# Linear-attention layers: the product of query and key sum moved from ScalarE to GpSimd, and a longer lag between blocks

## The chip, the cores and the metric

One core of a Trainium2 chip runs the whole program. The metric is the time on the device of one execution, in microseconds, as the median of several. The engines are named as in the profile: PE (TensorE's matmuls), PEld (its weight loads), DVE (VectorE), ACT (ScalarE), POOL (GpSimd), SP (SyncE, which issues the DMAs here).

## The reference

The program is a chain of twelve stages on x of shape 16 x 256 x 128: four "macaron" sandwiches, each half an FFN, an attention, half an FFN. The change touches one stage, the linear-attention layers (`attn1`), eight layers one after the other:

```python
for i in range(8):                       # 8 layers, 16 heads of 64
    residual = x
    Q  = elu(x @ Wq[i] + bq[i]) + 1
    Kf = elu(x @ Wk[i] + bk[i]) + 1
    V  = x @ Wv[i] + bv[i]
    KV, sumK = sum_s(Kf * V), sum_s(Kf)  # over the 256 positions of a sequence
    Z   = 1 / (Q * sumK + 1e-6)
    att = Q * KV * Z
    x = layer_norm(gelu(att @ Wo[i] + bo[i]) + residual) * ln1_s[i] + ln1_b[i]
    h = gelu(gelu(x @ W1[i] + b1[i]) @ W2[i] + b2[i])
    x = layer_norm(h + x) * ln2_s[i] + ln2_b[i]
```

## The kernel before

Everything is float32. A group is 512 tokens (`GT`), which is two sequences (`NQ`) of 256; there are 8 groups (`G`) and 8 layers, so 64 turns. The activations stay in SBUF, transposed (`zT`: 128 channels by tokens). The 1024 columns of heads are cut in 8 blocks (`NB1`) of 128, so that one block of one group is a tile of 128 x 512.

Each engine has its own program; they meet at semaphores only (`Ev` counts: `wait` asks that a step is done, `wait_free` that a buffer is free again). `over_layers` runs a list of parts in each slot, one slot for each group; a part has a lag, and in slot s it works on group s - lag. At the head of each pair of slots it calls `opening`, which on ACT loads the table set with exp and ln (L1790). The list is made at the end of `steps`: for each block position w from 0 to 7 it appends

- PE: `proj_pe(w)` (three matmuls, for keys, queries, values, L1488), then `out_pe(w - 3)` (L1502), which adds a block's attention times Wo into bank 6;
- ACT: `exp_act(w)` (exp of keys L1549, relu of keys L1550, exp of queries L1553), then `inv_act(w - 1)`: 1/(Q sumK + tiny) as exp(-ln(.)), one ln for each of the two sequences with the key sum as its scale (L1563), and one exp over 512 columns (L1568);
- DVE: `feature_dve(w)`: key feature and its sum, one instruction for each sequence (L1621), min(exp, 1) - 1 of the queries (L1629), max with q + b (L1632), values times key features and their sum (L1638, twice); then `att_dve(w - 2)`: Q times KV times Z (L1652, twice);
- POOL: `query_pool(w - 1)`: adds the 1 to the query features (L1690).

A negative block index wraps to the last blocks of the group before. At w = 2, when the last block of the group before has been added, the MLP is appended: on PE `mlp_pe` (L1515, L1521; for the group two slots back), on ACT the load of the gelu table (L1573), `y_act` (L1579, for the group one slot back), `h_act` (L1588, L1592) and the load of the exp table (L1596), on POOL the two residual additions (L1698, L1702). At w = 3 follow the transposes and norm statistics (L1529, L1663, L1668), at w = 4 POOL's reciprocal roots (L1711, L1714), at w = 5 the norm's application on DVE (L1677), at w = 6 the transposes back (L1538) and ACT's copies `back_act` (L1605, L1609). Weights of the next layer are loaded by SP while a layer runs.

The ring buffers of the attention are four deep (`a1_qf`, `a1_ksum`, `a1_kv`, `a1_z`, `a1_att`), those of the exponentials and key features two.

## Time and profile before

| | us |
|---|---|
| median of 3 runs (lowest, highest) | 6160.44 (6157.66, 6160.94) |
| the profiled execution | 6133.33 |
| its span, first to last instruction | 6131.5 |
| linear-attention layers within the span | about 1390 to 4277 |

The profiled execution is one of its own, 27 us below the median. The page gives each engine's busy time over the whole span; the linear-attention layers are slices 10 to 28 of its 40. A timeline row gives the start of an instruction in us from the span's start, its length, how many of the kind follow each other, and in brackets how long the engine sat idle before it and who released it. Instructions of one engine overlap a little, so that a pair of 0.48 us each may take 0.88 together.

### The profile page before, as it was taken

To read this page: it belongs to the slowest core of one execution; us is meant where nothing else is said; L and a number is where in the kernel's file an instruction comes from. 1 tells how busy PE (TensorE), PEld (TensorE's weight loads), DVE (VectorE), ACT (ScalarE), POOL (GpSimd) and SP (SyncE) were. 2 spreads that over 40 slices of the span, in tenths; PEclk is the share of its full clock that TensorE was granted. 3 is DMA by queue.
4 is the path that set the end of the run, shared out by engine and by line. 5 is a ranking of instruction groups with operands and counts; after the bars stand their busy time and mean duration, and the time that the engine had idled before them with its cause. 6 is when DMAs were issued, how large, how long until landed. Compare 5 with 4: busy or idle time off the path is not lost.

```text
span 6131.5 us, 75002 instructions
## 1 busy us (share of the span) xinstructions
PE 4957.9 (81%) x19882; PEld 2885.5 (47%) x19882; DVE 3793.3 (62%) x11610; ACT 2984.0 (49%) x5250; POOL 1120.8 (18%) x1540
## 2 busy tenths in 40 slices
PE   4788888848888888888888888888587559999964
PEld 2677777733333333333333333333354336665543
DVE  4555445567767667676677667676656744444466
ACT  1100000018878777787777878777122124444421
POOL 1000000022222222222222222222200012322210
PEclk8888888869999999999999999999798679999976
DMA  1000000000000000000000000000000023222300
GB/s 45 1 1 1 1 1 1 1 18 1 1 18 1 14 4 11 7 1 18 0 14 4 5 13 1 18 0 0 0 0 0 0 31 47 45 42 40 47 1 14
DMA packets 161144, 71.60 MB, mean 12 GB/s; under 512 B 64565, under 2 KB 158474, under 8 KB 160650
## 3 DMA queue, kind: packets, MB, share of 16 engines
q1 hardware_dynamic: 160778, 67.65, 6.4%
q8 instruction: 117, 1.92, 0.1%
q14 instruction: 249, 2.04, 0.1%
HBM read 55.89 MB, written 11.73 MB: 11 GB/s over the span
## 4 chain that ended last, share of the span: by engine, by line
PE 48%; DVE 24%; issue 13%; ACT 8%; SPq 3%; DMA 2%; POOL 1%; DVEq 1%; ACTq 0%; POOLq 0%
PE bank L1488 7%; PE bank L1521 4%; PE bank L1502 4%; PE bank L1210 3%; DVE arena L1652 3%; DVE arena L1638 3%; PE bank L1515 3%; SPq L2048 3%; PE bank L2107 3%; PE bank L1207 3%; PE bank L2167 3%; DVE arena L1621 2%; PE bank L1199 2%; DVE arena L1277 2%; DVE arena L1663 2%
## 5 line engine op out<-in xcount | busy, mean ns | idle before, releaser
L1488 PE MATMUL bank<-arena 128*128 (+1 forms) x3072 | 1474.1, 617 | 14.7 <-ACT arena L1550 13.1
L1488 PEld LDWEIGHTS bank<-arena 128*128 128x128 f32 x3072 | 599.4, 199 | 745.2 <-issue 710.0
L1621 DVE SCALAR_TENSOR_TENSOR arena<-arena 128x256 f32<-128x256 f32 x1024 | 391.8, 421 | 777.5 <-ACT arena L1550 773.3
L1502 PE MATMUL bank<-arena 128*128 128x512 f32 x1024 | 566.4, 636 | 219.2 <-DVE arena L1652 217.9
L1563 ACT ACTIVATE arena<-arena,const_table 128x256 f32<-128x256 f32 x1024 | 558.7, 601 | 78.9 <-POOL arena L1690 78.8
L1690 POOL TENSOR_SCALAR arena<-arena 128x512 f32<-128x512 f32 x512 | 316.7, 619 | 1356.7 <-DVE arena L1632 1349.3
L1638 DVE SCALAR_TENSOR_TENSOR arena<-bank,bv,arena 128x256 f32<-128x256 f32 x1024 | 450.4, 478 | 0.0
L1652 DVE SCALAR_TENSOR_TENSOR arena<-arena 128x256 f32<-128x256 f32 x1024 | 448.7, 480 | 0.7 <-issue 0.7
L2118 DVE TENSOR_REDUCE arena<-bank 128x2 f32<-128x512 f32 x256 | 176.9, 691 | 419.8 <-PE bank L2109 419.7
L1502 PEld LDWEIGHTS bank<-arena 128*128 128x128 f32 x1024 | 168.2, 191 | 556.6 <-DVE arena L1652 501.9
L1549 ACT ACTIVATE arena<-bank,bqk 128x512 f32<-128x512 f32 x512 | 350.0, 684 | 162.6 <-PE bank L1488 129.6
L1632 DVE SCALAR_TENSOR_TENSOR arena<-bank,bqk,arena 128x512 f32<-128x512 f32 x512 | 384.4, 751 | 18.1
L2151 ACT ACTIVATE arena<-bank 128x512 f32<-128x512 f32 x256 | 152.9, 597 | 479.1 <-PE bank L2140 479.1
L1515 PE MATMUL bank<-arena 128*128 128x512 f32 x512 | 283.7, 683 | 118.6 <-ACT arena L1588 117.6
L1553 ACT ACTIVATE arena<-bank,bqk 128x512 f32<-128x512 f32 x512 | 352.2, 688 | 8.9 <-PE bank L1488 8.6
L1550 ACT ACTIVATE arena<-bank,bqk 128x512 f32<-128x512 f32 x512 | 347.9, 680 | 0.5 <-issue 0.5
L1568 ACT ACTIVATE arena<-arena 128x512 f32<-128x512 f32 x512 | 322.7, 630 | 16.2
L2107 PE MATMUL bank<-const_table,arena 128*128 128x256 f32 x1024 | 324.1, 410 | 3.4 <-issue 2.1
L1277 DVE TENSOR_TENSOR arena<-arena,bank 128x512 f32<-128x512 f32 x352 | 227.6, 685 | 136.7 <-PE bank L1210 136.7
L2094 POOL TENSOR_TENSOR arena<-arena 128x256 f32<-128x256 f32 x256 | 185.4, 724 | 647.4 <-DVE arena L2084 647.4
L332 ACT ACTIVATE xT<-bank 128x512 f32<-128x512 f32 x64 | 38.2, 597 | 510.1 <-PE bank L327 479.5
L1210 PE MATMUL bank<-arena 128*128 128x128 f32 x1536 | 281.1, 276 | 0.0
(340 smaller groups left out, 8923.2 us busy)
## 6 DMA issues: line engine op xcount, KB each, us to landing
arena<-packed_dram SPq DMA_DIRECT2D x432, 64.0 KB
packed_dram<-arena SPq DMA_DIRECT2D x48, 192.0 KB, 2.1
arena<-in_L_attn_Wk_dram SPq DMA_DIRECT2D x16, 256.0 KB, 3.0
arena<-in_L_attn_Wq_dram SPq DMA_DIRECT2D x16, 256.0 KB, 3.8
arena<-in_L_attn_Wv_dram SPq DMA_DIRECT2D x16, 256.0 KB, 4.3
arena<-in_L_attn_Wo_dram SPq DMA_DIRECT2D x8, 512.0 KB, 3.5
arena<-in_L_attn_W_dram SPq DMA_DIRECT2D x16, 256.0 KB, 2.9
out_dram<-x SPq DMA_DIRECT2D x1, 2048.0 KB, 8.7
```

The lines of the kernel that those rows point to most:

```text
L1210: last = nc.tensor.matmul(bank[:, 4 + 3 * c, h * P:(h + 1) * P], a0_X[:, c, h, :], a0_It[:, c, h, :] if k else ident, start=True, stop=True)
L1277: last = nc.vector.tensor_tensor(dst[:, c, :, :], old, four(bank[:, 3 + i + 3 * c, :]), ALU.subtract)
L1488: nc.tensor.matmul(bank[:, RING1[m % 5], :], w1p[k][:, i * P:(i + 1) * P], zT_of(g), start=True, stop=True).then_inc(a1_proj.sem, 1)
L1502: nc.tensor.matmul(bank[:, 6, :], wo1[:, i, :], a1_att[:, i % 4, :], start=(i == 0), stop=(i == NB1 - 1)).then_inc(a1_outd.sem, 1)
L1515: nc.tensor.matmul(bank[:, i % 2, :], w1a[:, i * P:(i + 1) * P], a1_x1[:], start=True, stop=True).then_inc(a1_h_psum.sem, 1)
L1553: nc.scalar.activation(a1_eq[:, i % 2, :], q, ACT.Exp, bias=bqk[:, 1, i:i + 1])\
L1563: last = nc.scalar.activation(seqs(a1_z[:, i % 4, :])[q], seqs(a1_qf[:, i % 4, :])[q], ACT.Ln, bias=table[:, C_TINY:C_TINY + 1], scale=a1_ ...
L1621: last = nc.vector.scalar_tensor_tensor(seqs(a1_kf[:, i % 2, :])[q], seqs(a1_ek[:, i % 2, :])[q], 1.0, seqs(a1_kf[:, i % 2, :])[q], ALU.mi ...
L1632: nc.vector.scalar_tensor_tensor(a1_qf[:, i % 4, :], b[1], bqk[:, 1, i:i + 1], a1_eq[:, i % 2, :], ALU.add, ALU.max)\
L1638: last = nc.vector.scalar_tensor_tensor(seqs(a1_kv_terms[:])[q], seqs(b[2])[q], bv1[:, i:i + 1], seqs(a1_kf[:, i % 2, :])[q], ALU.add, ALU ...
L1652: last = nc.vector.scalar_tensor_tensor(seqs(a1_att[:, i % 4, :])[q], seqs(a1_qf[:, i % 4, :])[q], a1_kv[:, i % 4, q:q + 1], seqs(a1_z[:, ...
L2107: nc.tensor.matmul(dst, a3_R[:, w % 4, i * P:(i + 1) * P], table[:, C_KEYS:C_KEYS + T], start=True, stop=False)
```

## The change

The two logarithms of a block, which took the key sum as their scale, become one logarithm over 512 columns without a scale, in place in `a1_z`. Its argument, the query feature times the key sum, is now made by POOL in `query_pool`: behind its addition of 1 it waits for that, and multiplies each of the two sequences by its key sum with a pointer operand (`a1_qs` tells ACT). The wait for a free buffer moves from ACT to POOL, and DVE gets one more, ahead of L1632. The lags along the blocks grow by one: `inv_act(w - 2)`, `att_dve(w - 3)`, `out_pe(w - 4)`; `query_pool(w - 1)` keeps its own. The MLP and all that follows it move from w = 2, 3, 4, 5, 6 to w = 3, 4, 5, 6, 7.

```diff
--- before.py
+++ after.py
@@ -1405,6 +1405,7 @@
             a1_kfd = ev("a1_kfd", per=NB1)
             a1_qmin = ev("a1_qmin", per=NB1)
             a1_qfd = ev("a1_qfd", per=NB1)
+            a1_qs = ev("a1_qs", per=NB1)
             a1_ln = ev("a1_ln", per=NB1)
             a1_inv = ev("a1_inv", per=NB1)
             a1_attd = ev("a1_attd", per=NB1, credit=4, by="vector")
@@ -1557,13 +1558,9 @@
                 def inv_act(i):
                     def fn(g, u):
                         t = turn(g)
-                        a1_qfd.wait(nc.scalar, t, i + 1)
-                        a1_attd.wait_free(nc.scalar, t, i + 1)
-                        for q in range(NQ):
-                            last = nc.scalar.activation(seqs(a1_z[:, i % 4, :])[q], seqs(a1_qf[:, i % 4, :])[q],
-                                                        ACT.Ln, bias=table[:, C_TINY:C_TINY + 1],
-                                                        scale=a1_ksum[:, i % 4, q:q + 1])
-                        last.then_inc(a1_ln.sem, 1)
+                        a1_qs.wait(nc.scalar, t, i + 1)
+                        nc.scalar.activation(a1_z[:, i % 4, :], a1_z[:, i % 4, :], ACT.Ln,
+                                             bias=table[:, C_TINY:C_TINY + 1]).then_inc(a1_ln.sem, 1)
                         a1_ln.wait(nc.scalar, t, i + 1)
                         nc.scalar.activation(a1_z[:, i % 4, :], a1_z[:, i % 4, :], ACT.Exp, scale=-1.0)\
                             .then_inc(a1_inv.sem, 1)
@@ -1629,6 +1626,7 @@
                         nc.vector.tensor_scalar(a1_eq[:, i % 2, :], a1_eq[:, i % 2, :], 1.0, -1.0, ALU.min, ALU.add)\
                             .then_inc(a1_qmin.sem, 1)
                         a1_qmin.wait(nc.vector, t, i + 1)
+                        a1_attd.wait_free(nc.vector, t, i + 1)
                         nc.vector.scalar_tensor_tensor(a1_qf[:, i % 4, :], b[1], bqk[:, 1, i:i + 1],
                                                        a1_eq[:, i % 2, :], ALU.add, ALU.max)\
                             .then_inc(a1_read["q"].sem, 1)
@@ -1688,6 +1686,13 @@
                         a1_read["q"].wait(nc.gpsimd, t, i + 1)
                         apart(nc.gpsimd)
                         nc.gpsimd.tensor_scalar(a, a, 1.0, 1.0, ALU.add, ALU.mult).then_inc(a1_qfd.sem, 1)
+                        a1_qfd.wait(nc.gpsimd, t, i + 1)
+                        a1_attd.wait_free(nc.gpsimd, t, i + 1)
+                        apart(nc.gpsimd)
+                        for q in range(NQ):
+                            last = nc.gpsimd.tensor_scalar(seqs(a1_z[:, i % 4, :])[q], seqs(a)[q],
+                                                           a1_ksum[:, i % 4, q:q + 1], 1.0, ALU.mult, ALU.mult)
+                        last.then_inc(a1_qs.sem, 1)
                     return fn
 
                 def residual_pool(i):
@@ -1723,24 +1728,24 @@
 
                 for w in range(NB1):
                     pe.append((0, proj_pe(w)))
-                    of(pe, out_pe, w - 3)
+                    of(pe, out_pe, w - 4)
                     act.append((0, exp_act(w)))
-                    of(act, inv_act, w - 1)
+                    of(act, inv_act, w - 2)
                     dve.append((0, feature_dve(w)))
-                    of(dve, att_dve, w - 2)
+                    of(dve, att_dve, w - 3)
                     of(pool, query_pool, w - 1)
-                    if w == 2:
+                    if w == 3:
                         pe.append((2, mlp_pe))
                         act += [(1, gelu_table_act), (1, y_act), (2, h_act), (1, exp_table_act)]
                         pool += [(1, residual_pool(0)), (2, residual_pool(1))]
-                    if w == 3:
+                    if w == 4:
                         pe += [(1, turn_in_pe(0)), (2, turn_in_pe(1))]
                         dve += [(1, norm_stats_dve(0)), (2, norm_stats_dve(1))]
-                    if w == 4:
+                    if w == 5:
                         pool += [(1, norm_rstd_pool(0)), (2, norm_rstd_pool(1))]
-                    if w == 5:
+                    if w == 6:
                         dve += [(1, norm_dve(0)), (2, norm_dve(1))]
-                    if w == 6:
+                    if w == 7:
                         pe += [(1, turn_back_pe(0)), (2, turn_back_pe(1))]
                         act += [(1, back_act(0)), (2, back_act(1))]
                 return pe, act, dve, pool
```

## Rows read from the trace of the kernel before

**Rows 1.** The page's part 1: busy us (share of span) xinstructions.

```profile
PE 4957.9 (81%) x19882; PEld 2885.5 (47%) x19882; DVE 3793.3 (62%) x11610; ACT 2984.0 (49%) x5250; POOL 1120.8 (18%) x1540
```

**Rows 2.** Stretches: start:end, length, busy (x) PE, PEld, DVE, ACT, POOL, clock, DMA, GB/s.

```profile
1390.00:4277.00 2887.00, 2516.68 (x6084) 1077.12 (x6083) 2057.09 (x7682) 2292.99 (x3729) 642.47 (x887) 0.95 0.03 7
3006.85:3010.26 3.41, 3.36 (x8) 1.44 (x8) 3.37 (x12) 3.01 (x7) 0.62 (x1) 1.00 0.00 0
3013.80:3025.56 11.76, 10.45 (x21) 4.51 (x22) 0.00 (x1) 6.48 (x10) 3.11 (x3) 0.85 0.00 0
3058.45:3068.51 10.06, 8.75 (x21) 3.91 (x22) 0.00 (x0) 6.47 (x10) 3.12 (x3) 1.00 0.00 0
```

**Rows 3.** Waits in the stage, who for whom: us in total, times, longest.

```profile
DVE arena L1621 <- ACT arena L1550: 773.3, 129, 11.8
```

**Rows 4.** Timeline of DVE and PE around two holes.

```profile
3025.56 0.43 DVE L1621 SCALAR_TENSOR_TENSOR arena<-arena 128x256 f32<-128x256 f32 x1 [11.76 <-ACT arena L1550]
...
3068.51 0.43 DVE L1621 SCALAR_TENSOR_TENSOR arena<-arena 128x256 f32<-128x256 f32 x1 [10.06 <-ACT arena L1550]
...
3015.11 3.62 PE L1515 MATMUL bank<-arena 128*128 128x512 f32 x4 [1.94 <-ACT arena L1588]
```

**Rows 5.** Timeline of ACT and DVE around the table load of a second group.

```profile
2996.23 0.78 ACT L1609 ACTIVATE arena<-bank,bd 128x512 f32 x1 [0.60 <-PE bank L1538]
...
3000.49 1.28 ACT L1790 ACT_TABLE_LOAD   x1
...
2998.63 0.42 DVE L1621 SCALAR_TENSOR_TENSOR arena<-arena 128x256 f32<-128x256 f32 x1
...
3003.34 0.42 DVE L1621 SCALAR_TENSOR_TENSOR arena<-arena 128x256 f32<-128x256 f32 x1 [1.22 <-ACT arena L1550]
```

**Rows 6.** Timeline of ACT and PE from the last block into the MLP.

```profile
3010.72 1.09 ACT L1563 ACTIVATE arena<-arena,const_table 128x256 f32<-128x256 f32 x2
3011.85 0.63 ACT L1568 ACTIVATE arena<-arena 128x512 f32<-128x512 f32 x1
...
3013.80 0.69 ACT L1579 ACTIVATE arena<-bank,bd 128x512 f32<-128x512 f32 x1
...
3010.44 1.02 PE L1502 MATMUL bank<-arena 128*128 128x512 f32 x2
```

**Rows 7.** POOL's operations by line: duration ns min/median/max.

```profile
L1690 POOL TENSOR_SCALAR arena<-arena x512: 617/617/628, 1393.9 to 4273.1; 128x512 f32<-128x512 f32 x171
...
L1711 POOL TENSOR_SCALAR arena<-arena x128: 193/201/448, 1440.3 to 4308.8; 128x4 f32<-128x4 f32 x128
...
L2094 POOL TENSOR_TENSOR arena<-arena x256: 721/724/762, 5006.2 to 5873.5; 128x256 f32<-128x256 f32 x128
```

**Rows 8.** One plain block on DVE and POOL; then L1652 as a group.

```profile
3005.97 0.88 DVE L1652 SCALAR_TENSOR_TENSOR arena<-arena 128x256 f32<-128x256 f32 x2
...
3007.45 0.42 DVE L1629 TENSOR_SCALAR arena<-arena 128x512 f32<-128x512 f32 x1
...
3005.44 0.62 POOL L1690 TENSOR_SCALAR arena<-arena 128x512 f32<-128x512 f32 x1 [4.10 <-DVE arena L1632]
...
L1652 DVE SCALAR_TENSOR_TENSOR arena<-arena 128x256 f32<-128x256 f32 x1024 | 448.7, 480 | 0.7 <-issue 0.7
```

**Rows 9.** Places where DVE and POOL hold each other up.

```profile
3031.97 0.43 POOL L1711 TENSOR_SCALAR arena<-arena 128x4 f32<-128x4 f32 x1
...
3031.92 0.42 DVE L1621 SCALAR_TENSOR_TENSOR arena<-arena 128x256 f32<-128x256 f32 x1
...
1450.49 0.62 POOL L1690 TENSOR_SCALAR arena<-arena 128x512 f32<-128x512 f32 x1 [4.39 <-DVE arena L1632]
...
1450.71 1.07 DVE L1652 SCALAR_TENSOR_TENSOR arena<-arena 128x256 f32<-128x256 f32 x2
...
5362.18 0.73 POOL L2094 TENSOR_TENSOR arena<-arena 128x256 f32<-128x256 f32 x1 [2.13 <-DVE arena L2084]
...
L276 DVE TENSOR_SCALAR zn<-xn,meanvar,rstd x96: 315/342/802, 1302.5 to 5696.1; 128x128 f32<-128x128 f32 x96
```

## The prediction

> **What bounds the kernel now.** I read the page first: PE is the busiest engine over the whole span, DVE is next, POOL is nearly empty [rows 1]. That average mixes twelve stages, so the second view is the table of stretches. The linear-attention layers fill 2887 us of the 6131.5. One plain block of 3.41 us has PE busy for 3.36 and DVE for 3.37, ACT for 3.01 and POOL for 0.62; in the 11.76 us after the last block of a pair of projections and MLP, DVE does nothing [rows 2]. So a group (512 tokens) has two kinds of time: blocks that DVE paces, with PE as tight, and a hole in which PE and ACT pass the MLP back and forth.
>
> The waits say the same. DVE's idle time in this stage is nearly all one wait, L1621 for ACT's L1550, 773.3 us [rows 3]. Of the 773.3, 62 waits are holes: 32 of 10.06 to 10.19 us and 30 of 11.76 (the two rows shown stand for them); PE's granted clock over the two shown is 1.00 and 0.85 of 2.4 GHz, and in the longer one four L1515 take 3.62 us from 3015.11, at the lower of its two levels (1.2 GHz), after a pause of 1.94 us [rows 2, 4]; together 676 us. The other 97 us lie in 67 short waits, of which some 31 are the 1.22 us behind the table load that opens every second group [rows 5].
>
> What sets the hole is a chain. DVE's last L1652 of a block releases the out matmul, behind which the next-but-one block's projections stand in PE's order; then ACT makes its exponentials, logarithms (L1563) and inverse (L1568), loads the gelu table, does y and h, and after the MLP loads the other table and makes the exponentials of the next block, whose end lets DVE start [rows 4, 6]. ACT's logarithms and inverse stand ahead of that table load, without a pause between them. So the anchor of a hole is DVE's end two blocks before it; the work of DVE in those two blocks is free, that of the other six of a group is not.
>
> **Part 1, one logarithm of 512 columns for two of 256.** The two take 1.09 us, from 3010.72 to 3011.81, and L1568, an activation of the same 128x512 from the same memory, takes 0.63 [rows 6]. I take 0.63 for the new one: 0.46 less per block. In plain blocks ACT is not the bound, so that is worth nothing. In the block ahead of the MLP it moves the table load and all behind it forward: 62 x 0.46 = 29 us less. (y also waits for the last out matmul, which ends at 3011.46, 2.3 us before y starts, so that doesn't stop it [rows 6].)
>
> **Part 2, the table load of every second group.** Before, ACT's two back_act copies (L1609 ends at 2997.01), the block of 3.5 us and then the load follow each other, and DVE idles 1.22 us [rows 5]. With all lags one longer, the copies stand right ahead of the load. ACT then starts L1549 at 2997.01 + 1.28 = 2998.3 and ends the second activation 1.25 later, at 2999.5. DVE would be ready at 2998.63, where its next L1621 starts now [rows 5]. The idle time is 0.9 for 1.22: 31 x 0.3 = 9 us less. The bounds are 0 and 0.46 (0 to 14 us).
>
> **Part 3, the multiplication on POOL.** Added per block: a wait for POOL's own L1690 and two tensor_scalar of 128x256 with a pointer to the key sum. No row has a pointer operand on POOL. L1690 takes 0.617 for 512 columns and L1711, the same operation, 0.201 for 4, so a column costs (0.617 - 0.201)/508 = 0.82 ns and 256 columns 0.41 us [rows 7]. The nearest dearer row is L2094, 0.724 for 256 columns with two tensor inputs [rows 7]. I take 0.41, since the operation and its one tensor are L1690's. POOL would be busy some 1.5 of 3.4 us, which alone costs nothing: its result is used by ACT one block later than before. ACT's pauses for L1690 disappear, but DVE had no idle time of them.
>
> What costs is where the two land. L1690 ends at 3006.05, so they start near 3006.2, while DVE runs L1652, L1652, L1621, L1621, L1629 without a gap until 3007.9 [rows 8]. Today L1690 runs beside L1638, and stays at 617 to 628 ns in all 512 [rows 7, 8]. But three cases show that the two engines can exclude each other [rows 9]. POOL behind DVE: L1711, 0.201 by itself, takes 0.43 from 3031.97 when L1621 runs, and ends 0.06 after L1621's recorded end (3032.34), though DVE's next instruction follows at once. So POOL gets in between two DVE instructions. DVE behind POOL: at 1450.71 the pair of L1652 takes 1.07 for 0.88; it could start 0.19 late, at 1450.90, 0.21 before L1690's recorded end (1451.11). The same where L2094 starts among L276: the longest of those is 802 ns against a median of 342.
>
> From these: a POOL operation of 256 columns that waited for a DVE instruction ends 0.06 + 252 x 0.82 ns = 0.26 after that one's end; the next DVE instruction can start 0.21 before that, at +0.05, while in the plain pair it starts at -0.08 (two of 0.48 in 0.88). So each such collision costs DVE 0.13 to 0.14 us. The first multiplication meets the first L1652 and delays the second; the second one meets that and delays L1621 of the next block. Of the six blocks that count, six have the first collision, and three the second: behind two of them norm statistics or norm_dve follow, which read PSUM, and the sixth's falls behind the anchor. That is 62 x 9 = 558, less two in each of 31 groups that the idle time of part 2 swallows: 496 x 0.14 = 69 us more. Bounds: 0, if POOL waits until DVE's L1632 instead; with 0.724 each collision is 0.45, 558 x 0.45 = 251 less 31 x 0.9 = 28 swallowed, so 223.
>
> The Trainium skill, "SBUF — State Buffer", section "Who interferes with whom", says that a DVE instruction with two SBUF inputs contends with GpSimd's reads, that the first to issue keeps the shared pair for its whole instruction, and that the other fully blocks. L1711 and L1652 agree that the other blocks; that DVE may start 0.21 before POOL's recorded end makes the collision 0.14 and not the whole 0.41, by which the sum would hold about 496 x 0.35 = 174 us, an estimate from that page's rule.
>
> **Part 4, the rest.** DVE's new wait ahead of L1632 asks for L1652 of four blocks before, the last DVE work of the previous block, so it is over; queued behind it are L1632 and L1638, and POOL and ACT wait for those. L1652 has three waits ahead of it and 0.7 us of idle time in 1024 [rows 8]. I take nothing, and by that row both bounds are below 1 us. The longer lags move the MLP, norm and back steps one block later on all queues with unchanged order among them; weights' loads keep their distance. The very last group has one more inverse and multiplication behind its last projection: 1 us.
>
> **Sum.** -29 - 9 + 69 + 1 = +32 us. The profiled execution took 6133.3 us and would take 6165. The median of the runs shown is 6160.4, 27 above it, so I forecast 6192 us as the median.
>
> **Rivals.** (a) Faster: POOL's multiplications don't hold up DVE, because they slip in at L1632 and L1638. For it: L1690 stands beside L1638 in every block without being longer, and L1652's mean is its plain 480 ns [rows 7, 8]. Against it: they don't start there, and L1711 didn't wait for L1632. Time: 6160 - 29 - 9 + 1 = 6123. It decides where a collision costs below 0.08 us (38/496). Chance 0.22. (b) Much slower: the pointer form on POOL costs what L2094 costs: 6160 - 37 + 223 = 6346. Chance 0.15. (c) The clock: 30 of 62 holes ran 1.7 us longer at half clock. PE's pause ahead of the third L1515 shrinks by 0.46, so it may be granted full clock in all: 51 us less, 6141 with the port's cost; the plain blocks, stretched by 0.14 to 0.28, speak against it and could give all 62 the long hole, 6192 + 32 x 1.7 = 6246. 0.10 for the first; the second lies in the range. (d) The two effects cancel: a collision at half its cost (0.07) gives 6158. Chance 0.09. That the shorter logarithm fails to reach the hole, 6221, I put into the slower part. Forecast: 0.44.
>
> **How the numbers follow.** A measurement of this kernel can tell about 0.2%, 12 us, from no change. Faster: (a) and most of (c), 0.28. Same: (d) and the edges of the neighbours, 0.14. Slower: the forecast and (b), 0.58. The range of 6118 to 6290 takes in (a), (c), and collisions up to 0.35 us (a multiplication of 0.62, as long as L1690); it leaves out the top of (b). For the likeliest case alone it is 6165 to 6225.
>
> **What would show it.** Right: L1563's group has 512 of about 630 ns; the holes are 9.6 and 11.3; the new POOL line has 1024 of at least 0.41 us, many longer, since they wait; L1652's mean rises from 480 ns by some 70 and its maximum is common; L1621's rises less. Wrong: L1652 and L1621 keep 480 and 421 ns (then a); the POOL line's shortest is above 0.5 us (then b); ACT's idle time ahead of L1549 doesn't grow, though ACT has 0.46 less to do; DVE waits ahead of L1652 for L1568.

## The result and the profile after

The change makes the kernel slower: the median of four runs is 6207.9 us (6184.2 to 6213.4), that of the kernel before 6159.1 us beside them (6141.7 to 6160.9). The ratio is 1.0087, with an interval of 1.0059 to 1.0115, so some 50 us were lost. I had forecast 6192, in a range of 6118 to 6290. The profiled execution of after took 6184.2 us, that of before 6133.3: again 51 us apart, so the two profiles show the whole of the loss. One execution of the kernel before beside the experiments took 6634 us at a mean granted clock of 0.74, and it is left out of every comparison.

The page of the kernel after, part 1 (busy us, share of span, instructions), and of its part 5 the groups that answer to [rows 6 to 8] (busy, mean ns of one, idle before and its releaser). Code lines moved: L1618 was L1621, L1650 was L1652, L1688 was L1690, L1562 is the new logarithm, L1550 was L1549, L1551 was L1550, and L1693 is new.

```profile
PE 4957.3 (80%) x19882; PEld 2863.7 (46%) x19882; DVE 3948.0 (64%) x11610; ACT 2804.7 (45%) x4738; POOL 1772.5 (29%) x2564
...
L1618 DVE SCALAR_TENSOR_TENSOR arena<-arena 128x256 f32<-128x256 f32 x1024 | 452.2, 477 | 669.3 <-ACT arena L1551 652.8
...
L1693 POOL TENSOR_SCALAR arena<-arena 128x256 f32<-128x256 f32 x1024 | 652.1, 647 | 116.7 <-POOL arena L1688 116.7
...
L1550 ACT ACTIVATE arena<-bank,bqk 128x512 f32<-128x512 f32 x512 | 351.0, 686 | 491.9 <-PE bank L1489 446.0
L1650 DVE SCALAR_TENSOR_TENSOR arena<-arena 128x256 f32<-128x256 f32 x1024 | 540.5, 570 | 0.3 <-issue 0.3
...
L1562 ACT ACTIVATE arena<-arena,const_table 128x512 f32<-128x512 f32 x512 | 372.2, 727 | 0.0
```

The rows of before that these answer to and that did not stand ahead of the prediction:

```profile
L1621 DVE SCALAR_TENSOR_TENSOR arena<-arena 128x256 f32<-128x256 f32 x1024 | 391.8, 421 | 777.5 <-ACT arena L1550 773.3
...
L1563 ACT ACTIVATE arena<-arena,const_table 128x256 f32<-128x256 f32 x1024 | 558.7, 601 | 78.9 <-POOL arena L1690 78.8
...
L1549 ACT ACTIVATE arena<-bank,bqk 128x512 f32<-128x512 f32 x512 | 350.0, 684 | 162.6 <-PE bank L1488 129.6
```

DVE runs exactly as many instructions as before (11610), but is busy for 3948.0 us where it was 3793.3 [rows 1]: 154.7 us more. They are nearly all in two lines. L1650 went from a mean of 480 ns [rows 8] to 570, that is 92 us in 1024; L1618 from 421 to 477, that is 57. L1636, which also works on 256 columns but reads PSUM, still has its 478. ACT has 179 us less to do, and its wait for PE at L1550 grew from 129.6 to 446.0 us: it is ahead and waits for the others.

The other side of the account is the hole. The rows are the waits of the stage, then one hole on the timeline of DVE, then that stretch among the stretches (columns as in rows 2).

```profile
DVE arena L1618 <- ACT arena L1551: 647.5, 113, 9.7
...
3049.31 0.46 DVE L1618 SCALAR_TENSOR_TENSOR arena<-arena 128x256 f32<-128x256 f32 x1 [9.23 <-ACT arena L1551]
...
3040.08:3049.31 9.23, 8.75 (x21) 3.92 (x22) 0.00 (x1) 5.64 (x9) 3.57 (x5) 1.00 0.00 0
```

The longest wait is 9.7 us where it was 11.8 [rows 3]. Before, 32 of 62 holes took 10.06 to 10.19 us and 30 took 11.76; after, 51 take 9.2 and ten 9.7, and none is long. Summed in the two traces from DVE's first key feature (L1618) to its last L1650, its idle time in holes fell from 675 to 577 us and the rest of its idle time from 153 to 142. So +155 - 99 - 11 = +45, and that stretch did grow by 45 us, from 2885.4 to 2930.7. From the first to the last key exponential, the length that is used below, the stage went from 2879.2 to 2921.2 us, 42 more. The other 6 to 9 of the 51 lie outside it, where executions of the same kernel also differ.

What the 155 us are is seen in one plain block. First DVE's timeline, then POOL's, over the same 2.5 us.

```profile
2842.09 1.09 DVE L1650 SCALAR_TENSOR_TENSOR arena<-arena 128x256 f32<-128x256 f32 x2
2843.11 0.41 DVE L1618 SCALAR_TENSOR_TENSOR arena<-arena 128x256 f32<-128x256 f32 x1
...
2843.45 0.60 DVE L1618 SCALAR_TENSOR_TENSOR arena<-arena 128x256 f32<-128x256 f32 x1
...
2843.99 0.42 DVE L1626 TENSOR_SCALAR arena<-arena 128x512 f32<-128x512 f32 x1
...
2841.57 0.62 POOL L1688 TENSOR_SCALAR arena<-arena 128x512 f32<-128x512 f32 x1 [5.46 <-DVE arena L1630]
2842.41 1.38 POOL L1693 TENSOR_SCALAR arena<-arena 128x256 f32<-128x256 f32 x2 [0.23 <-POOL arena L1688]
```

The two products start 0.23 us behind L1688, while DVE runs L1650, and end at 2843.79. The pair of L1650 takes 1.09 for its plain 0.88 [rows 8]: the second one gives way to the first product. The second product waits for DVE in turn, 0.89 us for an operation that takes 0.48 when nothing is in its way, and L1618 behind it is 0.60 for 0.42. L1626 has its plain 0.42 again.

The next table is worked out from the traces, as means over the 61 whole groups between two holes: each row is one of DVE's instructions in a group's eight blocks, counted from the hole, in ns.

```
block after the hole        0    1    2    3    4    5    6    7
before L1652 second       478  479  478  479  479  479  479  479
after  L1650 second       699  613  699  699  689  696  693  479
after  L1618 second       604  422  529  419  492  594  573  570
(L1621 second, before: 421 to 427 in every block)
```

The first product meets DVE in seven of eight blocks and costs some 220 ns in six of them, 134 in the second block after the hole. The second product's cost varies more: 150 to 180 ns of L1618 in four blocks, 108 and 72 in two others, and some of L1626.

### The profile page after: what moved, and what is told of

It is laid out like the page before. It is cut to its first block, busy times and chain, and to the rows that moved or that the text cites. A ratio compares the mean times of both kernels' runs of the same rounds, so it can differ in the third digit from the quotient of the medians.

```text
span 6182.4 us, 76646 instructions
## 1 busy us (share of the span) xinstructions
PE 4957.3 (80%) x19882; PEld 2863.7 (46%) x19882; DVE 3948.0 (64%) x11610; ACT 2804.7 (45%) x4738; POOL 1772.5 (29%) x2564
## 4 chain that ended last, share of the span: by engine, by line
PE 39%; DVE 30%; issue 16%; ACT 6%; SPq 3%; DMA 2%; POOL 2%; DVEq 1%; ACTq 0%; POOLq 0%
DVE arena L1650 6%; DVE arena L1636 4%; PE bank L1522 4%; DVE arena L1618 3%; PE bank L1210 3%; SPq L2053 3%; PE bank L1207 3%; PE bank L2112 3%; PE bank L2172 2%; DVE arena L1675 2%; DVE arena L1626 2%; PE bank L1516 2%; PE bank L1199 2%; PE bank L1489 2%; PE bank L1503 2%
## 5 line engine op out<-in xcount | busy, mean ns | idle before, releaser
L1618 DVE SCALAR_TENSOR_TENSOR arena<-arena 128x256 f32<-128x256 f32 x1024 | 452.2, 477 | 669.3 <-ACT arena L1551 652.8
L1693 POOL TENSOR_SCALAR arena<-arena 128x256 f32<-128x256 f32 x1024 | 652.1, 647 | 116.7 <-POOL arena L1688 116.7
L1688 POOL TENSOR_SCALAR arena<-arena 128x512 f32<-128x512 f32 x512 | 316.6, 618 | 899.1 <-DVE arena L1630 889.8
L1550 ACT ACTIVATE arena<-bank,bqk 128x512 f32<-128x512 f32 x512 | 351.0, 686 | 491.9 <-PE bank L1489 446.0
L1650 DVE SCALAR_TENSOR_TENSOR arena<-arena 128x256 f32<-128x256 f32 x1024 | 540.5, 570 | 0.3 <-issue 0.3
L1636 DVE SCALAR_TENSOR_TENSOR arena<-bank,bv,arena 128x256 f32<-128x256 f32 x1024 | 450.5, 478 | 0.0
L1562 ACT ACTIVATE arena<-arena,const_table 128x512 f32<-128x512 f32 x512 | 372.2, 727 | 0.0
L1551 ACT ACTIVATE arena<-bank,bqk 128x512 f32<-128x512 f32 x512 | 347.7, 679 | 0.0
```

What stands on the lines that cost most here:

```text
L1562: nc.scalar.activation(a1_z[:, i % 4, :], a1_z[:, i % 4, :], ACT.Ln, bias=table[:, C_TINY:C_TINY + 1]).then_inc(a1_ln.sem, 1)
L1618: last = nc.vector.scalar_tensor_tensor(seqs(a1_kf[:, i % 2, :])[q], seqs(a1_ek[:, i % 2, :])[q], 1.0, seqs(a1_kf[:, i % 2, :])[q], ALU.mi ...
L1636: last = nc.vector.scalar_tensor_tensor(seqs(a1_kv_terms[:])[q], seqs(b[2])[q], bv1[:, i:i + 1], seqs(a1_kf[:, i % 2, :])[q], ALU.add, ALU ...
L1650: last = nc.vector.scalar_tensor_tensor(seqs(a1_att[:, i % 4, :])[q], seqs(a1_qf[:, i % 4, :])[q], a1_kv[:, i % 4, q:q + 1], seqs(a1_z[:, ...
L1693: last = nc.gpsimd.tensor_scalar(seqs(a1_z[:, i % 4, :])[q], seqs(a)[q], a1_ksum[:, i % 4, q:q + 1], 1.0, ALU.mult, ALU.mult)
```

## The experiments

Three theories stood against each other. The forecast's: DVE and POOL exclude each other, and a meeting costs DVE the POOL operation's length less a fixed part. The first rival: a meeting has a fixed price, so fewer operations are cheaper. The second: the longer lags cost time, and the products are only beside it. For the gain, the shorter logarithm and the lags had to be told apart. Each kernel was timed against the kernel before on the same chip; ratios are those. Beside them stand DVE's busy time and the length of the stage (first to last key exponential), both from the one profiled execution:

```
                           ratio   interval          stage us   DVE busy   long holes
before                     1                         2879.2     3793.3     30
after                      1.0087  1.0059 to 1.0115  2921.2     3948.0      0
lags alone                 0.9988  0.9961 to 1.0014  2861.4     3793.6     10
no product                 0.9878  0.9860 to 0.9896  2815.4     3793.5      0
one log, old lags          0.9901  0.9867 to 0.9936  2799.8     3794.2      0
constant product           1.0024  1.0001 to 1.0047  2904.9     3914.3      0
one product of 512         1.0168  1.0138 to 1.0198  2962.2     3982.7      0
two logs again             1.0130  1.0100 to 1.0159  2942.2     3947.8      0
products timed             0.9993  0.9968 to 1.0018  2866.4     3835.5      0
folded, in the window      0.9932  0.9906 to 0.9958  2833.8     3832.3      0
folded, not in the window  1.0043  1.0019 to 1.0067  2891.3     3919.0      0
folded, one pointer        0.9884  0.9847 to 0.9922  2819.4     3826.3      0
```

The rest of the span, where these kernels are the same, was 3252 us in the profile of before, 3304 in that without products and 3227 in that of the timed products: a profiled time may lie 40 us off its kernel's median for reasons outside the stage, and the stage's own length is the better measure of a profile.

**The lags alone.** The kernel before with the longer lags and DVE's new wait, everything else as before.

```
  (the change's lags and its wait_free ahead of a1_qf, without these:)
- last = nc.gpsimd.tensor_scalar(seqs(a1_z...)[q], seqs(a)[q], a1_ksum[...], 1.0, MULT, MULT)
- nc.scalar.activation(a1_z, a1_z, ACT.Ln, ...)
+ two nc.scalar.activation(seqs(a1_z)[q], seqs(a1_qf)[q], ACT.Ln, scale=a1_ksum[...])
```

> The kernel before with the longer lags alone (and DVE's extra wait for a free buffer): two logarithms with the key sum as scale stay on ACT, POOL keeps its single addition. Theory (shared access of DVE and POOL is what costs): DVE's instructions keep 421 and 480 ns, the time is within 15 us of before's 6160. Rival (the lags cost: ACT's table load now stands right behind its copies, and DVE has one more wait): this kernel alone shows most of the 49 us, about 6200.

Measured: 0.9988 (0.9961 to 1.0014), DVE busy 3793.6 us. By the ratio the lags and the added wait cost nothing that can be told, and bring nothing. In the profile two things cancel: 52 holes took 10.1 us and 10 took 11.8, which is 34 us less than before, while DVE's idle time outside the holes was 172 us for before's 153.

**The gain without the product.** After, with POOL's products left out and the logarithm of 512 taken straight from the query features.

```
- for q in range(NQ): nc.gpsimd.tensor_scalar(... a1_ksum[...], 1.0, MULT, MULT)
- nc.scalar.activation(a1_z, a1_z, ACT.Ln, ...)
+ nc.scalar.activation(a1_z, a1_qf, ACT.Ln, ...)
```

> The changed kernel without POOL's two multiplications: ACT takes one logarithm of 512 columns of the query features, so the key sum is left out of the inverse (part of the computation is missing). Theory: DVE back at 421 and 480 ns, holes still near 9.7 us and mostly at full clock, time 6160 - 23 (0.36 us in each of 64 holes) - up to 51 (clock) = 6085 to 6137. Rival (the lags cost): not below 6190.

Measured: 0.9878 (0.9860 to 0.9896), 75 us less than before. DVE busy is 3793.5, and L1650 and L1618 are back at 479 and 420 ns. Here is one hole on DVE's timeline, and L1562 and L1650 from part 5 of the page.

```profile
2985.32 0.43 DVE L1618 SCALAR_TENSOR_TENSOR arena<-arena 128x256 f32<-128x256 f32 x1 [9.70 <-ACT arena L1550]
...
L1650 DVE SCALAR_TENSOR_TENSOR arena<-arena 128x256 f32<-128x256 f32 x1024 | 448.3, 479 | 1.2 <-issue 1.2
...
L1562 ACT ACTIVATE arena<-arena,const_table 128x512 f32<-128x512 f32 x512 | 372.3, 727 | 0.0
```

All 62 holes are 9.7 us and none is long. So the gain is larger than I had it (75 for 38), and the products' cost, from this kernel to after, is 1.0087 - 0.9878 = 0.0209, or 128 us (some 20 either way, by the two intervals), and 106 by the stage's length, where I had 69. DVE's account gives 155 us of longer instructions, less 25 in the holes and 23 in other idle times that they fill: 107.

**The gain with the old lags.** The kernel before, with the logarithm of 512 and without the factor.

```
  (as above, and the lags of before:)
- of(pe, out_pe, w - 4)   of(act, inv_act, w - 2)   of(dve, att_dve, w - 3)
+ of(pe, out_pe, w - 3)   of(act, inv_act, w - 1)   of(dve, att_dve, w - 2)
```

> The kernel before with its old lags and without a product: ACT takes one logarithm of 512 columns of the query features with no scale (the key sum is left out of the inverse). e2_no_product is the same with the longer lags and took 6074, 75 us below before. Theory (the gain is ACT's shorter work ahead of the table load, the lags give nothing): 6060 to 6095. Rival (the longer lag is what lets ACT use its shorter logarithm): 6120 to 6150.

Measured: 0.9901 (0.9867 to 0.9936), holes 9.7 us, none long. The intervals of this kernel and of the one above overlap, so the gain is seen with the old lags too, and my 9 us for the table load are not seen in a ratio. In the profiles the longer lags cost something: DVE's idle time outside the holes is 146 us here and 165 in the kernel above, the same 19 us as between before (153) and the lags alone (172).

**The product with a constant.** After, with 1.0 in place of the pointer to the key sum.

```
- a1_ksum[:, i % 4, q:q + 1], 1.0, ALU.mult, ALU.mult)
+ 1.0, 1.0, ALU.mult, ALU.mult)
```

> The changed kernel with POOL multiplying by the constant 1.0 for the pointer to the key sum (the key sum is left out of the inverse). Theory: the multiplication's own length falls from 498 ns (the shortest tenth in the changed kernel) to about 410, and with it each collision from some 0.22 to 0.14 us: L1650's mean from 570 to about 540 ns, DVE's busy time some 50 us below the changed kernel's, time about 6175. Rival (the number of collisions counts, not the length of POOL's instruction): DVE's lengths and the time stay as in the changed kernel, 6208.

Measured: 1.0024 (1.0001 to 1.0047), 39 us under after. The first row is the line's own view (ns min/median/max), the others are of part 5.

```profile
L1693 POOL TENSOR_SCALAR arena<-arena x1024: 406/442/573, 1393.1 to 4300.9; 128x256 f32<-128x256 f32 x171
...
L1618 DVE SCALAR_TENSOR_TENSOR arena<-arena 128x256 f32<-128x256 f32 x1024 | 449.9, 474 | 686.8 <-ACT arena L1551 675.6
...
L1650 DVE SCALAR_TENSOR_TENSOR arena<-arena 128x256 f32<-128x256 f32 x1024 | 511.8, 541 | 0.4 <-issue 0.4
```

With constants the shortest product takes 406 ns, which is what I had worked out from L1690 and L1711 [rows 7]. The same view of after shows what the pointer adds:

```profile
L1693 POOL TENSOR_SCALAR arena<-arena x1024: 476/635/1009, 1392.4 to 4316.5; 128x256 f32<-128x256 f32 x171
```

476 for 406, 70 ns. Counted by blocks as in the table of the first section, a first meeting costs 139 ns here (L1650's second takes 618 for 479). So the 0.14 us of the prediction was right for a product of 0.41 us; the product was not of that length. Even so the products cost 90 us in this kernel (1.0024 - 0.9878, and the stage's lengths say 90 too), not 69. The same count by blocks finds some 15 of these 21 us: the six blocks that count have 0.86 us of first meetings, where I had 6 x 0.14 = 0.84, but 0.56 of second ones, where I had 3 x 0.14 = 0.42, and the last two blocks, which I took as free, give back only 0.33 us of their 0.42 in a shorter hole.

**One product of 512.** After, with a single product, scaled by the first sequence's key sum.

```
- for q in range(NQ): nc.gpsimd.tensor_scalar(seqs(a1_z...)[q], seqs(a)[q], a1_ksum[:, i % 4, q:q + 1], ...)
+ nc.gpsimd.tensor_scalar(a1_z[:, i % 4, :], a, a1_ksum[:, i % 4, 0:1], 1.0, ALU.mult, ALU.mult)
```

> The changed kernel with one multiplication of 512 columns by the first sequence's key sum for the two of 256 (the second sequence gets a wrong key sum). By the rows so far a meeting costs DVE the length of POOL's instruction less 0.27 us: one of about 0.69 us costs 0.42, two of 0.49 cost 2 x 0.22. Theory (length counts): DVE's busy time about as in the changed kernel, within 30 us, time 6190 to 6215. Rival (each meeting has a fixed price of 0.22): DVE some 75 us less busy, time about 6145.

Measured: 1.0168 (1.0138 to 1.0198), DVE busy 3982.7, both above what I expected. DVE's timeline in one block, then POOL's:

```profile
2909.30 1.31 DVE L1650 SCALAR_TENSOR_TENSOR arena<-arena 128x256 f32<-128x256 f32 x2
...
2909.61 0.72 POOL L1692 TENSOR_SCALAR arena<-arena 128x512 f32<-128x512 f32 x1 [0.23 <-POOL arena L1688]
```

A single meeting per block now costs 0.43 us (1.31 for 0.88), and L1618's mean is back at 421. A fixed price for each meeting is refuted: there are fewer, and the whole is dearer. Three lengths give one line. Shortest product 406, 476, 690 ns; first meeting 139, 220, 434 ns. The difference is 267, 256 and 256: in these three kernels a meeting costs the POOL operation's length less 0.26 us. (A kernel further down, with two pointers, does not lie on this line.)

**Two logarithms again.** After, with the logarithm as two of 256 without a scale.

```
- nc.scalar.activation(a1_z[:, i % 4, :], a1_z[:, i % 4, :], ACT.Ln, bias=...)
+ for q in range(NQ): nc.scalar.activation(seqs(a1_z...)[q], seqs(a1_z...)[q], ACT.Ln, bias=...)
```

> The changed kernel with the product on POOL, but two logarithms of 256 columns on ACT again, without a scale. Nothing is left out. Theory: each hole is 1.09 - 0.73 = 0.36 us longer, 64 x 0.36 = 23 us; if PE's longer pause in the MLP also brings back the lower clock in half of the holes, up to 50 us more: 6230 to 6280. Rival (DVE alone sets the time, the logarithm is hidden): 6208.

Measured: 1.0130 (1.0100 to 1.0159), 26 us over after. The stage grew by 21. The line's own view (ns min/median/max):

```profile
L1563 ACT ACTIVATE arena<-arena,const_table x1024: 492/512/528, 1398.5 to 4339.8; 128x256 f32<-128x256 f32 x171
```

That is 512 for L1563's 601 in before: the scale by a pointer had made them long. The holes grew by 0.2 us, 13 us in 62, and the other idle times by 7. The long holes, which I had put as possible, did not come back.

**The same products, placed elsewhere.** Nothing left out: the products of a block run one block later, behind DVE's L1626 of the next block, where DVE reads PSUM for some 1.7 us.

```
+ def product_pool(i):      # of(pool, product_pool, w - 2)
+     a1_qmin.wait(nc.gpsimd, t, i + 2)
+     (the two products, as in after)
```

> The changed kernel with the same two multiplications, with their pointers, one block later on POOL: they wait for DVE's L1626 of the next block, so that they run beside L1630 and L1636, which have one input in SBUF. Nothing is left out. Theory: the multiplications keep their 0.5 us, their meetings with DVE shrink to one per block of at most 0.15 us (L1688 now ends later and can reach the first L1650); DVE's busy time at least 100 us below the changed kernel's, time about 6100 to 6130, faster than before. Rival (POOL's added work or the lags cost, wherever it stands): about 6200.

Measured: 0.9993 (0.9968 to 1.0018). DVE busy is 3835.5, 112 us under after, so the place takes three quarters of the growth away. In five of eight blocks the two products and L1688 fit beside DVE's reads of PSUM and cost DVE less than 20 ns. The 42 us that stay come from the other three, most of them from the second block after a hole: there POOL has the norm's own work ahead of the products, and L1688 slips to where DVE runs L1650. POOL's timeline there (L1700 are the products), then DVE's:

```profile
2846.15 0.94 POOL L1700 TENSOR_SCALAR arena<-arena 128x256 f32<-128x256 f32 x2
2847.06 0.78 POOL L1688 TENSOR_SCALAR arena<-arena 128x512 f32<-128x512 f32 x1
...
2846.80 1.32 DVE L1650 SCALAR_TENSOR_TENSOR arena<-arena 128x256 f32<-128x256 f32 x2
```

The pair takes 1.32 there. The ratio missed what I expected (6100 to 6130 us is 0.9926 to 0.9974), although DVE's part came out. In the stage it is 51 us over the kernel without products: 42 of DVE's work and 9 of idle time (ACT now waits for POOL, 91 us in all, most of it hidden). The profiled run, at 6095 the fastest of ten, owed part of that to what lies outside the stage, 25 us less than in before. By the ratios the distance is 71 us and not 51, and here the clock may count: the ten executions have a mean granted clock of 0.900 to 0.905, and the four slowest (6161 to 6163 us) have 0.900 or 0.901, as before has. The profile with no long hole is the one at 0.905, so it may not stand for the other nine.

**Less work, in the window.** Nothing left out: (q+1) is folded into the product, as q times key sum plus key sum, in place, so that L1688 falls away; the key-value column is divided by the key sum instead (a reciprocal of 128x2 on DVE, one small product on POOL). The products wait for DVE's minimum of the next block.

```
- nc.gpsimd.tensor_scalar(a, a, 1.0, 1.0, ALU.add, ALU.mult)
- (the two products into a1_z)
+ a1_qmin.wait(nc.gpsimd, t, i + 2)
+ nc.gpsimd.tensor_scalar(seqs(a)[q], seqs(a)[q], k, k, ALU.mult, ALU.add)
+ nc.gpsimd.tensor_tensor(a1_kvn, a1_kv, a1_rk, ALU.mult)     # a1_rk: nc.vector.reciprocal(a1_ksum)
```

> A version meant to keep the gain without the meetings; nothing is left out. POOL's addition of 1 is folded into the product ((q x key sum) + key sum, two of 256 columns, in place), started behind DVE's L1626-like minimum of the next block, so beside the two instructions of DVE that have one input in SBUF; since the attention then reads the product, its factor is KV divided by the key sum (a reciprocal of 2 columns on DVE, a multiplication of 2 columns on POOL). Theory: the last L1650-like instructions at 480 ns and L1618-like at 421 again, DVE's busy time within 60 us of before, time 6070 to 6110, against 6146 for before on that chip. Rival (POOL's products cost wherever they stand): above 6146.

Measured: 0.9932 (0.9906 to 0.9958). DVE busy is 3832.3, the 512 reciprocals of 154 ns among it, and L1661, which is L1650 of after, has a mean of 488 ns.

**The same without the window.** The same instructions, but the products right behind the maximum of their own block.

```
- a1_qmin.wait(nc.gpsimd, t, i + 2)       of(pool, query_pool, w - 2)
+                                         of(pool, query_pool, w - 1)
```

> e8_window with the products at the place of the changed kernel, right behind DVE's own maximum of the same block, without the wait for the next block's minimum; the same instructions on every engine, nothing left out. Theory (the place decides): the first product ends before DVE's next two-input instruction, the second stands in its way for about 0.35 us in every block: the L1661-like group's mean rises from 488 to 600 ns or more, DVE's busy time by 100 us or more, time 100 us or more above e8. Rival (the folded product is cheap because it is one POOL instruction less): within 20 us of e8.

Measured: 1.0043 (1.0019 to 1.0067), 68 us more than in the window, and 58 by the stage's length; less than I expected. Part 5's groups, then the timelines of POOL and DVE:

```profile
L1702 POOL TENSOR_SCALAR arena<-arena 128x256 f32<-128x256 f32 x1024 | 704.0, 696 | 664.9 <-DVE arena L1634 664.7
...
L1661 DVE SCALAR_TENSOR_TENSOR arena<-arena 128x256 f32<-128x256 f32 x1024 | 533.1, 562 | 0.4 <-issue 0.4
...
2907.15 1.34 POOL L1702 TENSOR_SCALAR arena<-arena 128x256 f32<-128x256 f32 x2 [0.42 <-DVE arena L1634]
...
2907.66 1.10 DVE L1661 SCALAR_TENSOR_TENSOR arena<-arena 128x256 f32<-128x256 f32 x2
```

The first product fits beside DVE's reads of PSUM, the second does not: one meeting of 219 ns in six of eight blocks, 64 x 6 x 0.219 = 84 us, which is DVE's growth of 87. Only the place and the wait that sets it were changed between these two kernels, so it is the place that costs. The price itself is off the line above: the shortest product here takes 554 ns, which less 0.26 would be 0.29 us. In the trace this product ends 0.345 us behind the first L1661 of the pair, just where the product of after (one pointer, 476 ns) ends behind the first L1650, and both cost 0.22. So the second pointer made the operation longer and this meeting no dearer.

**The window with the shorter form.** The folded product in the window again, written as (q + 1.0) times key sum: one pointer for two.

```
- nc.gpsimd.tensor_scalar(seqs(a)[q], seqs(a)[q], k, k, ALU.mult, ALU.add)
+ nc.gpsimd.tensor_scalar(seqs(a)[q], seqs(a)[q], 1.0, k, ALU.add, ALU.mult)
```

> e8_window with the product written as (q + 1.0) x key sum, one pointer operand for two; nothing is left out. In e8 the product with two pointers took 555 ns and with one, in e4, 480. Theory (length of POOL's instruction matters only where it meets DVE, and in the window it hardly does): L1703 falls to about 480 ns, the time moves by less than 15 us from e8's 0.9932 of before. Rival (POOL's latency counts): about 30 us faster.

Measured: 0.9884 (0.9847 to 0.9922), 6073.8 us. It is the fastest complete kernel here, 1.2% under before and 2.0% under after. Its groups in the stage (columns as in part 5), and the products on POOL's timeline with the L1661 that follows on DVE's:

```profile
L1661 DVE SCALAR_TENSOR_TENSOR arena<-arena 128x256 f32<-128x256 f32 x1024 | 452.2, 483 | 0.8 <-issue 0.8
...
L1703 POOL TENSOR_SCALAR arena<-arena 128x256 f32<-128x256 f32 x1024 | 479.2, 478 | 1099.1 <-DVE arena L1630 983.7 <-issue 115.2
...
2929.53 0.93 POOL L1703 TENSOR_SCALAR arena<-arena 128x256 f32<-128x256 f32 x2 [2.38 <-DVE arena L1630]
...
2930.83 0.87 DVE L1661 SCALAR_TENSOR_TENSOR arena<-arena 128x256 f32<-128x256 f32 x2
```

The products end at 2930.46, before DVE starts L1661, which has its plain length. With two pointers a product took 547 ns at the shortest, here 473. The two ratios are 29 us apart and the stages 14; the intervals overlap, and DVE's busy time differs by 6 us only, so how much the shorter form brings stays open. The ratios are as far apart as the rival of the expectation had them (30 us), beyond the 15 that I had allowed; the stages are within it.

## Why the prediction came out as it did

The direction, the mechanism and the range were right; the forecast of 6192 (6165 for the profiled execution) was 16 to 19 us short. That closeness is partly luck: two terms were wrong by more, with opposite signs, the price of the product and the clock, and a small one, the table load, had the wrong sign. In the stage the profiles give -22 for the logarithm, -51 for the long holes, +12 for idle times that the longer lags add and +107 for the products, which is +46 beside the 45 that the stretch of DVE's work grew by; I had -29, 0, -9 and +69.

**Part 3, the product's price (69 us, measured 106 in the stage, 128 by the ratios).** The wrong step is the length of the product, "I take 0.41, since the operation and its one tensor are L1690's". It is 0.41 with constants and 0.48 with the pointer. The working from length to cost held: the three lengths lie on one line, which gives 0.14 at 0.41 and 0.22 at 0.48. This is the difference between the kernel with constants and after: 16 us by the stage, 39 by the ratio. The other error is the second meetings, and the 90 - 69 = 21 us of the kernel with constants are about its size. By the table the six blocks that count have 1.23 us a group of first meetings (I had 6 x 0.14 = 0.84) and 0.70 us of second meetings, in L1618 and L1626 (I had 3 x 0.14 = 0.42). 62 x 1.93 = 120 us, of which idle times swallow 23 (I had 62 x 0.14 = 9). The blocks that I took as free nearly were so: the meetings of the last two blocks, 0.5 us, are why most holes are 9.2 in after and 9.7 without products; of their 31 us the holes give back 25. The Trainium skill, "SBUF — State Buffer", section "Who interferes with whom", has the engine that comes second blocked for the whole of the other's instruction. The runs agree that it is blocked and that reads of PSUM are not (L1636 stays at 478), but the price is 0.26 us below the instruction's length at 406, 476 and 690 ns, and 0.33 below it at 554.

**Part 1, the logarithm (29 us, measured 23).** It takes 727 ns, where I took 630 from L1568. A hole gets 0.36 us shorter (10.06 to 9.70), and 62 x 0.36 is 22 to 23. Part of what made the two old logarithms long was the pointer as scale, 601 against 511 ns for 256 columns, and not their being two.

**The clock, rival (c) (51 us, chance 0.10).** This is the larger half of the gain, and it stood in the prediction as a rival with the right size. The two views of PE's MLP matmuls, of before and of after (busy, mean | idle before them):

```profile
L1515 PE MATMUL bank<-arena 128*128 128x512 f32 x512 | 283.7, 683 | 118.6 <-ACT arena L1588 117.6
...
L1516 PE MATMUL bank<-arena 128*128 128x512 f32 x512 | 248.7, 609 | 78.3 <-ACT arena L1585 77.3
```

The same 512 matmuls took a mean of 683 ns and take 609. Their pause for ACT went from 117.6 / 62 = 1.90 us to 1.25, and to 1.52 (94.0 / 62) without products. No profile of a kernel with the logarithm of 512 has a long hole. Together 22 + 51 = 73 us, of which 12 go to the idle times that the lags add: the stage of the kernel without products is 64 us shorter than before's, and its ratio shows 75 (some 11 either way). I had held the stretched blocks against this rival, and they did not bring the long hole back. But the pause does not decide alone: with the lags alone it is 1.88, as before, and there are 10 long holes for 30, at a time that is the same as before's within 0.3%. The counts are from one execution of each kernel, but the mean granted clock over the whole program is on record for single executions too. It is 0.897 to 0.902 in the 44 executions of before beside the experiments, and 0.904 to 0.912 in all 47 of the kernels with an unscaled logarithm, the timed products aside: 0.900 and 0.907 at the medians. Thirty holes of 11.76 us at 0.855 are 30 x 11.76 x 0.145 = 51 us of lost clock, or 0.008 of the span. So the ordinary executions differ by about what the thirty long holes are worth, and the gain is no accident of one profile; a mean over the program does not say where the clock was lost. The lags alone (0.900 to 0.907) and the timed products (0.900 to 0.905) lie between. What makes PE's clock fall in some holes and not in others stays open.

**Part 2, the table load (9 us less).** The step that failed is the new idle time of 0.9 for 1.22 us. Here is one such place in after (L1795 was L1790):

```profile
2652.73 1.28 ACT L1795 ACT_TABLE_LOAD   x1
...
2656.38 0.43 DVE L1618 SCALAR_TENSOR_TENSOR arena<-arena 128x256 f32<-128x256 f32 x1 [1.75 <-issue]
```

Over the 30 groups of this kind the mean is 1.74 us in before and 1.71 with the old lags and one logarithm, but 1.93 in after and 2.08 with the lags alone and without products: longer by 0.2 to 0.34 and not shorter by 0.3. I had worked it out from the time at which ACT is done with L1551 alone, but here L1551 had ended 1.1 us before this L1618 began, and what DVE waits for after that the trace does not say (issue). That DVE's idle time outside the holes is still 11 us less in after than in before is the products' doing, which fill it. The ratios of the old and the longer lags (0.9901 and 0.9878) do not tell them apart.

**Part 4 (0).** Held for the added wait: the lags alone give 0.9988, and L1650's idle time is 0.3 us in 1024.

**The signs to look for.** L1650's mean rose by 90 where I had said some 70, L1618's by 56, less as said. L1562 takes 727 ns where I had said 630. Holes of 9.6 and 11.3 did not appear, they are 9.2 and 9.7. ACT's idle time ahead of L1550 grew, as said, from 129.6 to 446.0. The shortest product was 476, under the 500 that would have spoken for rival (b). Rival (a), that the products slip in behind L1632, is what the change does not do and the three kernels with timed products do: 6123 was its forecast, and 0.9884 to 0.9993 of before, 6088 to 6155, is what they reach.

## What to carry to other kernels

Before work is given to an idle GpSimd, look at what VectorE runs at the moment when that work becomes ready, not at how idle GpSimd is: beside VectorE instructions that work on SBUF alone a meeting cost the bound engine a third to two thirds of the operation's length here (139 of 406 ns, 434 of 690), beside those that read PSUM next to nothing. A wait that holds the operation back until such a stretch, and a form that fits into it, turned 0.9% slower into 1.2% faster here. A price for an operation is taken from a row with the same kind of operands; a pointer in place of a constant was about half of the error in the largest term here. And a wait that one row puts down to one engine need not shrink when that engine comes earlier.

## What the runs showed of the hardware that I had not expected

- A tensor_scalar of 128x256 f32 on GpSimd takes 406 ns with two constants, 473 to 476 with one pointer, 547 to 554 with two: some 70 ns for each. Of 128x512 it takes 617 with constants and 690 with one pointer, so the addition is for the instruction and not for the column.
- On ScalarE a pointer as scale costs 90 ns (601 against 511 for a logarithm of 128x256).
- What VectorE loses where a GpSimd operation gets in between two of its instructions is the operation's length less 0.26 us, at 406, 476 and 690 ns (none or one pointer), but less 0.33 at 554 ns with two. In all four kernels VectorE's next instruction of 128x256 ends 0.27 us behind the GpSimd operation's recorded end.
- GpSimd gets in between two VectorE instructions that follow each other without a pause: in six of eight blocks the first product of after ends 0.345 us behind the first L1650, ahead of the second, and neither engine keeps the other out for longer than the one instruction.
- No hole was stretched by PE's lower clock in the profile of any kernel in which ACT's part of the hole was shorter than before, by 0.36 us or, with two unscaled logarithms, by less. In the profiles that was worth twice the shortening itself (51 us beside 22).
